# The shared expert's two layers move from a stage of their own into the combine stage

## The reference, cut to what matters

```python
def _expert_ffn(x, w1, b1, gate, w2, b2):
    h = jax.nn.gelu((x @ w1 + b1) * gate, approximate=False)
    return h @ w2 + b2
x = hidden_states
...
combine = jnp.sum(jax.nn.one_hot(topk_i, E, dtype=x.dtype) * topk_p[..., None], axis=-2)
moe = jnp.zeros_like(x)
for e in range(E):
    moe = moe + combine[..., e:e + 1] * _expert_ffn(x, w1[e], b1[e], gate[e], w2[e], b2[e])
shared = _expert_ffn(x, sw1, sb1, sgate, sw2, sb2) * jax.nn.sigmoid(shared_weight)
y = moe + shared
mu = jnp.mean(y, axis=-1, keepdims=True)
var = jnp.var(y, axis=-1, keepdims=True)
return (y - mu) * jax.lax.rsqrt(var + LN_EPS) * ln_g + ln_b
...
x = x + jnp.tanh(g_ffn[0]) * _L0_ffn_ref(_layernorm(x, axis=-1), ...)
```

## Time and profile before

| | before |
|---|---|
| median of three runs | 966.99 us (965.0 to 969.73) |
| the profiled execution, its own time | 970.94 us |
| its span | 968.9 us |
| PE busy | 701.2 us (72%) |
| VectorE (DVE) busy | 747.8 us (77%) |
| ACT busy | 539.0 us (56%) |
| POOL busy | 500.2 us (52%) |
| mean granted TensorE clock | 0.900 of full |

### The profile page before, as it was taken

The page is one execution under the profiler, slowest core; times in us unless marked ns, Lnnn a source line. Parts: engine busy times, 40 slices in busy tenths (PEclk is TensorE's granted clock), DMA queues, the critical chain, the costliest instruction groups (busy, mean ns, idle before and its releaser), DMA issues. The chain is left out here.

```text
span 968.9 us, 25824 instructions
## 1 busy us (share of the span) xinstructions
PE 701.2 (72%) x7850; PEld 563.9 (58%) x7851; DVE 747.8 (77%) x2277; ACT 539.0 (56%) x1099; POOL 500.2 (52%) x438
## 2 busy tenths in 40 slices
PE   2689788777788778787863469999999999990000
PEld 1456555555555555555541458899999999880000
DVE  5698999899989999988964388666665666654998
ACT  2777666756676665865531134455555556552654
POOL 5455567666666666666551692155455555541000
PEclk9999999999999999999885599999999999996555
DMA  4212112222122220300011711122222222225552
GB/s 115 63 39 51 45 50 52 67 62 54 35 65 62 62 54 33 92 26 15 29 40 39 238 36 38 31 68 74 68 74 68 73 69 70 70 68 140 155 150 87
DMA packets 90404, 66.19 MB, mean 68 GB/s; under 512 B 17008, under 2 KB 79728, under 8 KB 90352
## 3 DMA queue, kind: packets, MB, share of 16 engines
q1 hardware_dynamic: 69152, 35.49, 14.7%
q0 software_dynamic: 8448, 17.45, 5.5%
q10 hardware_dynamic: 12752, 12.58, 3.9%
HBM read 38.21 MB, written 23.09 MB: 63 GB/s over the span
## 5 line engine op out<-in xcount | busy, mean ns | idle before, releaser
L1277 POOL DMA_INDIRECT expert_results<-y,dest x136 | 135.3, 995 | 155.4 <-DVE y L1244 109.4
L1099 ACT ACTIVATE hT<-bank,b1g_c,gate_c 128x256 f32<-128x256 f32 x272 | 138.6, 563 | 112.6 <-PE bank L76 111.4
L834 POOL TENSOR_TENSOR prob<-prob,mx 128x1024 f32<-128x1024 f32 x64 | 121.6, 1900 | 148.1 <-DVE mx L536 148.0
L166 POOL DMA_INDIRECT expert_lists<-xn,slots x128 | 124.7, 974 | 67.1 <-issue 30.6
L1041 PE MATMUL bank<-w,hT 128*128 x1088 | 136.1, 278 | 7.4 <-issue 6.8
L366 PE MATMUL bank<-kbd,qg 128*64 128x256 f32 x1024 | 135.5, 405 | 5.5 <-DVE prob L529 3.1
L1041 PEld LDWEIGHTS bank<-w,hT 128*128 128x128 f32 x1088 | 127.0, 191 | 15.0 <-issue 15.0
L762 ACT ACTIVATE PT<-bank 128x512 f32<-128x512 f32 x128 | 70.8, 592 | 85.0 <-PE bank L377 77.9
L383 PE MATMUL bank<-w_att,aT 128*128 128x128 f32 x128 | 33.1, 343 | 94.3 <-issue 65.4
L529 DVE TENSOR_TENSOR prob<-bank,mask 128x512 f32<-128x512 f32 x128 | 85.8, 672 | 17.8 <-PE bank L366 16.0
L366 PEld LDWEIGHTS bank<-kbd,qg 128*64 128x64 f32 x1024 | 70.5, 144 | 46.0 <-issue 16.4
(11 more groups left out here) (176 smaller groups left out, 1639.5 us busy)
## 6 DMA issues: line engine op xcount, KB each, us to landing
rows<-expert_lists SPq DMA_DIRECT2D x70, 130.0 KB
yin<-expert_results SPq DMA_DIRECT2D x16, 512.0 KB, 5.3
x_all<-in_x SPq DMA_DIRECT2D x16, 256.0 KB
ctx_in<-in_ctx SPq DMA_DIRECT2D x16, 256.0 KB
pad_k<-in_mask_BxS_ik SPq DMA_DIRECT2D x16, 256.0 KB
xn2T<-x2T ACTq DMA_DIRECT2D x16, 256.0 KB
out<-res ACTq DMA_DIRECT2D x7, 512.0 KB, 4.7
expert_results<-y,dest POOLq DMA_INDIRECT x136
```

Source lines behind the costliest of these rows:

```text
L166: po.indirect_dma_start(lists[:, :], bass.IndirectOffsetOnAxis(ap=m.slots[:, par, t, k:k + 1], axis=0), m.xn2[:, par, t, :], None).then_in ...
L834: po.tensor_tensor(ps, ps, mx[:, u, :].unsqueeze(2).broadcast_to([P, H, S]), ALU.subtract).then_inc(subbed, 1)
L1099: ac.activation(hT[:, par, c, :], h_ps[par][c // 2][:, (c % 2) * SL:(c % 2 + 1) * SL], ACT.Gelu, bias=b1g_c[:, c, bass.ds(e, 1)], scale=ga ...
L1277: po.indirect_dma_start(results[:, :], bass.IndirectOffsetOnAxis(ap=dest[:, par, h, :], axis=0), y[:, par, h, :], None).then_inc(sent[par] ...
```

## The change

The shared expert leaves the `experts` block. In `combine`, PE computes its first layer from `xn2T` and `sw1` in plain float32 (one product where there were three), ACT the Gelu, and PE the second layer into four PSUM banks (`sy_ps`), which `share` reads in place of `xn2T`. The shared expert's second bias is added to the eight experts' biases instead (once, on `b2_row`; a token's two weights sum to one). The last bias is added to `x_all` by VectorE, two quads in each of the first eight expert steps (`add_bias`, now on VectorE), so VectorE's list has eight steps written out ahead of its loop. The wait for `w1` is split in two halves.

```diff
-        def iterations(eng, body):
+        def iterations(eng, body, head=1):
             n = eng.value_load(pairs[0:1, 0:1], min_val=TOK // SL, max_val=(T - 3) // 2)
-            body(0, 0, 0)
-            body(1, 1, 0)
-            with eng.Fori(1, n) as i:
+            for i in range(head):
+                body(i * 2, 0, i)
+                body(i * 2 + 1, 1, i)
+            with eng.Fori(head, n) as i:
...
-            for q in range(4):
-                table(q)
-                split_tokens(q + 2, q % 2)
-                keep(q, q % 2)
+            for part in range(4):
+                table(part)
             ve.wait_ge(biases_in, 48)
             ve.tensor_tensor(b1g_c[:, :, :], b1g_c[:, :, :], gate_c[:, :, :], ALU.mult).then_inc(biases_ready, 1)
...
+            ve.tensor_tensor(b2_row[:, :, :], b2_row[:, :, :], sb2_row[:, :].unsqueeze(1).broadcast_to([P, E, D]),
+                             ALU.add).then_inc(biases_ready, 1)
+            for es in range(E):
+                ve.wait_ge(w1_in[2 * es // E], 16)
+                split(ve, (w_split, lambda: ve.wait_ge(w_split, es * 2 + 1)), w1[:, es, 0, :].bitcast(F32R),
+                      w1[:, es, 1, :].bitcast(F32R), w1[:, es, 1, :])
...
+                if isinstance(t, int) and t < HEAD:
+                    for q in range(t * NQ // HEAD, (t + 1) * NQ // HEAD):
+                        add_bias(q)
...
+                ve.tensor_tensor(xs, xs, m.ln_row[:, 1, :].unsqueeze(1).broadcast_to([P, QT, D]), ALU.add)
+            iterations(ve, body, HEAD // 2)
...
-            with po.Fori(0, NQ) as q:
-                add_bias(q)
...
+        @block.tensor
+        def _(pe):
+            def hidden(q):
+                for c in range(SC):
+                    if q >= 2:
+                        pe.wait_ge(sh_gelued, (q - 2) * SC + c + 1)
+                    pe.matmul(sh_ps[q % 2][c][:, :], sw1[:, c * P:(c + 1) * P], xn2T[:, q * QW:(q + 1) * QW],
+                              start=True, stop=True).then_inc(sh_done, 1)
+            def shared(q):
+                pe.wait_ge(sh_gelued, q * SC + SC)
+                if q >= 4:
+                    pe.wait_ge(acc_step, (q - 4) // 2 * A_STEPS + (q % 2 + 1) * QT)
+                for t in range(QT):
+                    for c in range(SC):
+                        last = pe.matmul(sy_ps[q % 4][:, t * D:(t + 1) * D], hs[:, q % 2, c, t * P:(t + 1) * P],
+                                         sw2[:, c, :], start=(c == 0), stop=(c == SC - 1))
+                last.then_inc(sy_done, 1)
+            hidden(0)
+            for q in range(NGR * 2):
+                if q + 1 < NGR * 2:
+                    hidden(q + 1)
+                shared(q)
...
-                                        in1=shared[:, (g * GT + t) * D:(g * GT + t + 1) * D],
+                                        in1=sy_ps[(g * 2 + t // QT) % 4][:, t % QT * D:(t % QT + 1) * D],
...
+            def gelu(q):
+                if q >= 2:
+                    ac.wait_ge(sy_done, q - 1)
+                for c in range(SC):
+                    ac.wait_ge(sh_done, q * SC + c + 1)
+                    ac.activation(hs[:, q % 2, c, :], sh_ps[q % 2][c][:, :], ACT.Gelu, bias=scols[:, 2, c:c + 1],
+                                  scale=scols[:, 0, c:c + 1]).then_inc(sh_gelued, 1)
+            for g in range(2):
+                gelu(g * 2)
+                gelu(g * 2 + 1)
+                weigh(g)
             for g in range(NGR):
+                if g + 2 < NGR:
+                    gelu(g * 2 + 4)
+                    gelu(g * 2 + 5)
                 scale(g)
```

More of the change, by code:

```diff
@@ L978, in _ @@
             ident = cst[:, C_ID:C_ID + P]
[L981 to L1011, removed]
             def turn(t, par, i):
@@ L1064, in _ @@
             halves = [slice(k * E // 2, (k + 1) * E // 2) for k in range(2)]
-            for es in halves:
-                ac.dma_start(w1[:, es, 1, :], a["w1"][es].rearrange("e d f -> d e f")).then_inc(w1_in, 16)
+            for k, es in enumerate(halves):
+                ac.dma_start(w1[:, es, 1, :], a["w1"][es].rearrange("e d f -> d e f")).then_inc(w1_in[k], 16)
             for es in halves:
                 ac.dma_start(w2[:, es], a["w2"][es].rearrange("e (c f) d -> f e c d", f=P)).then_inc(w2_in, 16)
[L1069 to L1084, removed]
+            ac.wait_ge(biases_ready, 2)
             ac.wait_ge(table_ready, 1)
@@ L1171, in table @@
                     ve.tensor_copy(ends[:, :], count[:, :]).then_inc(table_ready, 1)
-            for q in range(4):
-                table(q)
-                split_tokens(q + 2, q % 2)
-                keep(q, q % 2)
+            for part in range(4):
+                table(part)
             ve.wait_ge(biases_in, 48)
             ve.tensor_tensor(b1g_c[:, :, :], b1g_c[:, :, :], gate_c[:, :, :], ALU.mult).then_inc(biases_ready, 1)
-            first = max(4, NQ - 2 - E)
-            for q in range(4, first):
-                split_tokens(q + 2, q % 2)
-                keep(q, q % 2)
-            ve.wait_ge(w1_in, 32)
-            es = 0
-            for q in range(first, NQ - 1):
-                if q + 2 < NQ:
-                    split_tokens(q + 2, q % 2)
-                keep(q, q % 2)
-                while es < E and (q == NQ - 2 or es * (NQ - 2 - first) < E * (q + 1 - first)):
-                    split(ve, (w_split, lambda: ve.wait_ge(w_split, es * 2 + 1)), w1[:, es, 0, :].bitcast(F32R),
-                          w1[:, es, 1, :].bitcast(F32R), w1[:, es, 1, :])
-                    es += 1
+            ve.wait_ge(shared_scaled, 4)
+            ve.tensor_tensor(b2_row[:, :, :], b2_row[:, :, :], sb2_row[:, :].unsqueeze(1).broadcast_to([P, E, D]),
[4 more added lines that the diff above has]
+                      w1[:, es, 1, :].bitcast(F32R), w1[:, es, 1, :])
             ve.wait_ge(w_split, 2 * E)
@@ L1290, in combine @@
     TOK = NT * P
-    x_all, shared, weight, ln_row = m.x_all, m.xn2T, m.weight, m.ln_row
+    SC = FS // P
+    x_all, xn2T, weight, ln_row = m.x_all, m.xn2T, m.weight, m.ln_row
+    sw1, sw2, scols, banks = m.sw1, m.sw2, m.scols, m.banks
     out_rows = out.rearrange("b s d -> (b s) d")
@@ L1304, in combine @@
         res = sb("res", [P, 2, GT, D])
+        hs = sb("hs", [P, 2, SC, QW])
+        sh_ps, sy_ps = [banks[0:2], banks[2:4]], banks[4:8]
+        sh_done, sh_gelued, sy_done = (sem("c_" + n) for n in ("sh_done", "sh_gelued", "sy_done"))
         y_in = [sem(f"y_in{i}") for i in range(2)]
```

48 lines of the change are left out of this document (11 added, 37 removed).

## The result

The changed kernel takes 941.09 us (median of 4 executions, 938.25 to 952.71). The kernel before took 968.36 beside it on the same chip (965.0 to 973.96). The difference of the medians is 27.3 us. The profiled execution took 941.31 us by its own time, with a span of 938.8, against 970.94 and 968.9 before. The forecast was 947.6 in a range of 937 to 961.

A forecast was written before the change was run, and what follows sets the result against it. PE was taken to bound the expert steps and VectorE `combine`. The terms -31.4 + 1.5 + 4 + 6.5 = -19.4 us took the median from 966.99 to 947.6 us, range 937 to 961.

The forecast's parts named there:

- Start of the expert steps: Ahead of the expert steps: the first product comes at 584.1 us against 615.48, -31.4 us.
- VectorE's splits block POOL's scatters: Ahead of the expert steps: eight splits each hold up a scatter, pads 4.9 us later, 952.5 us; chance 6%.
- PE cold at the start: First expert steps: PE, idle since attention, begins them at half clock, +1.5 us, from 0.5 to 3.
- The last bias: First eight expert steps: two additions per step on VectorE make steps of 4.33 us, +4 us, from 1 to 9.8.
- Combine, steady state: Groups of `combine`: PE's products and ACT's Gelus fit beside VectorE's 9.60 us, and `share` from PSUM costs nothing, 0 us.
- Head of combine: Start of `combine`: VectorE's fifth share waits for PE's cold first quads, +6.5 us, from 2 to 14.
- PE at half clock in `combine`: Rival in `combine`: PE sets the group at 15.0 us in place of 9.60, 985 us; chance 7%.
- ACT as the bound: Rival in `combine`: Gelus come late behind PE and cost 2.4 us a group, 965 us; chance 10%.
- That the change saves nothing there: Rival at the expert steps' start: the chain through SP ends just as late, 979 us; chance 2%.
- VectorE stopped again: Rival at the head of `experts`: VectorE's unexplained stop grows, the start loses 8 to 12 us more, 958 us; chance 10%.
- The 4.9 us that no row explained: Head of `experts` before: VectorE's wait ended at 559.08, though PE's second layer was over at 554.2.
- VectorE still waits over 10 us between attention and the first step: Between attention and the first expert step: a VectorE wait over 10 us would show the prediction wrong.

The follow-up runs named there:

- third set: Follow-up runs on one chip, the same as the first set's, beside the kernel before (median 944.44 us); the change itself was not run.
- bias run: The changed kernel with the last bias back on GpSimd and one pair of VectorE's steps written out; 969.68 us in the first set, 916.47 in the third set.
- run with late splits: The changed kernel with VectorE's splits of `w1` held until the pads are ready (one wait); 969.03 us, ratio 0.989 to the kernel before.
- first set: Follow-up runs on one chip beside the kernel before (median 986.29 us), on the bias, the shared expert, the splits and the written-out head.
- second set: Follow-up runs on one chip beside the kernel before (median 965.39 us); the only set with the change unaltered, at 942.73 us, ratio 0.975.
- last run: The changed kernel with pads ahead of the scatters, last-but-one quad's scatters at the end of attention, and last bias on GpSimd; 915.73 us, ratio 0.970.

## Why the prediction was right, point by point

**Start of the expert steps: -31.4 forecast, -31.75 measured** from the first scatter to the first product. In the third set the distance from the first scatter to the first `y` was 84.66 in the kernel before and 54.52 in the bias run, -30.1. The chain was read rightly, POOL's scatters and pads, then SP, with some terms that cancel. The pads were 0.8 us later behind the first scatter (27.60 for 26.77): the scatters took 2.2 us longer beside the splits, the `tensor_scalar` group 1.4 less (3.19; 4.57 was its time before). From SP's first rows to the first product it took 3.81 us, where 2.3 + 2.88 = 5.2 were forecast: before, a second layer of 1.95 us stood between PE's transposes and the first product. The marks that were named came as forecast, shifted by attention's 2.0 us: first pad 567.8 (565), first rows 581.9 (579), first product 585.7 (582 to 588).

**VectorE's splits block POOL's scatters** was a rival at +4.9 us. Its mechanism is real but smaller: 1.3 to 1.9 us by the run with late splits, with single scatters of 1.48 and 1.66 us for 0.96 beside splits. Two others of 1.35 and 1.24 us stand clear of the splits (544.36, 559.98), so something else slows them too.

**PE cold at the start: +1.5 forecast, 0 measured in the changed kernel.** Its first products do run at half clock, 0.21 us apart for 0.12 later. But before, the first step had gaps of 1.00 and 0.29 us in which PE waited for VectorE and ACT, and the slower products fill these. In the other profiles without the stage, first product to first `y` is 6.9 to 8.1 us, so 0 to 1.2.

**The last bias: +4 forecast, 2.5 measured** for the first eight steps (32.3 against 29.8). VectorE's step was forecast at 4.33 us and is 4.01. Against the later steps of its own profile (29.4) it is 2.9, and 4.65 at the pace of the third set. What it costs is 4.01 less the step that PE could do, so this term depends on that pace: the eight take 32.1 to 32.7 us in every profile that has it.

**Combine, steady state: 0 forecast, 0 measured.** Group 9.60 us as before, and without the shared expert the stage is no shorter than in the kernel before (94.32 us, 94.59). `share` with its operand in PSUM takes 340 ns (x64), with SBUF it took 344. The Trainium skill (VectorE: DVE Perf Modes, on the TRN2 errata) gives PSUM the larger fixed part; this kernel's own instruction now shows that it isn't there for this form.

**Head of combine: +6.5 forecast, +3.4 measured.** The mechanism is as forecast, the fifth share waits for PE. PE started with SP's loads, as forecast (847.62, 847.57), and 6.0 us behind the last `y`, as SP's loads did before. The size was off in two terms. From there to the end of quad 1's second layer 12.4 us were forecast and 10.7 measured (858.36): the first layers of two quads took 5.29 us for 6.6, because the granted clock was at full after 3.6 us of work (851.2) and not after 5.6, and the later pieces follow each other 0.1 to 0.2 us closer. So the first group is 3.2 us late for 4.9. And of the further 1.6 us for the second group 0.3 came: the additions L1295 of groups 0 and 1 stand 7.64 us apart (859.62, 867.26), 7.31 before, because PE's next four pieces took 7.0 us for 7.7 and VectorE needed them 6.8 us after the first group's, not 6.1.

**Not in the sum: -3.7 us in the steps**, made of +2.5 from the bias and -6.2 from faster later steps (29.3 to 29.4 us for eight, 29.8 before). The third set shows the same step in both codes, and the first the same undisturbed pair of steps. So this most likely belongs to the executions, not to the change; at the pace of the first profiles it isn't shown, as the kernel before wasn't profiled at it again. What makes the pace of a set is open. In the first set waits of VectorE at `rT` are named `remote` (17.6 us, six times, longest 3.7, in the 100 us from 700 on, without the shared expert), in the third there are none and PE is busy over 99.9%.

**The other rivals.** PE at half clock in `combine`: its clock is 1.00 over the group shown and it is done before VectorE needs it. Between groups the clock did fall to 0.5 once in mid-stage (892.6 to 895.7), which the prediction named as a sign of being wrong; PE had enough lead, and the groups stayed at 9.6 us. ACT as the bound: it keeps 1.26 us of 9.60 idle, and `scale` comes 0.30 us after its input. That the change saves nothing there: PE no longer keeps landed rows waiting.

VectorE stopped again: its longest wait ahead of the splits is 1.09 us, on a DMA. The 4.9 us that no row explained are not in every execution: in the third set the kernel before waits 11.88 us there and goes on at 546.26, 0.03 us behind PE's second layer (542.48 + 3.75). The first 7.4 of the old 16.06 us, up to that layer's start at 550.43, came through ACT, whose first Gelu started at 548.84, behind the issue of a weight load (539.03, 8.42 us) and a table load. The sign "VectorE still waits over 10 us between attention and the first step" did come by its words (24.29 us), but behind all of VectorE's work, for rows; it was worded too widely.

**The sum.** With these parts alone, -31.75 + 2.5 + 3.4 = -25.9 us were the change's own in the first pair of profiles; -19.4 was forecast. The 6.5 us between are the head (3.1), the bias (1.5), the cold start (1.5) and the earlier steps (0.4), each of which came out better than priced. The rest of the span's -30.1 is +2.0 in attention and -6.2 of pace, which aren't the change's: without them the measured time would have been some 4 us nearer to the forecast. In the third set the parts are, with the run without the shared expert for the first two and the bias run for the last, -31.1 + 4.0 + 3.7 = -23.4 us, and the second set's medians differ by 22.7. So 23 to 26 us are the change's own. The ways to be wrong were judged well in the main, but one chance doesn't fit its time: ACT as the bound at 965 us was counted as faster than 962.2.

## What to carry to other kernels

A stage is best moved to where its engine is idle under another engine's bound. Here PE's work went under VectorE's group of 9.60 us and cost only the first group's start. Before pricing such a move, find the last wait behind the stage and follow its queue: here 22 us of landed rows lay unused, and the next limit, pads that stood behind the scatters although SP needed them first, together with scatters that could be sent earlier, gave another 16.5 us. When work is moved between VectorE and GpSimd, look at which SBUF instructions then run side by side; two gains that are measured apart need not add.

## What was not expected of the hardware

- GpSimd's additions and VectorE's float32 conversions in SBUF hold each other up, but not evenly. In the kernel before they took turns: 23.85 us for the 16 additions for 19.54 alone, with conversions of at most 1.55 us beside them (0.42 alone). In the last run one conversion stood for all 16 additions, 20.16 us. The Trainium skill (SBUF — State Buffer, on who interferes with whom) describes an exclusive lock on a shared port that is held for one instruction. By that rule the conversion would have waited for one addition of some 1.2 us; why it waited for 16 is open. The memset above, 2.05 us with 2.07 beside it, agrees with the rule. That the loop is the cause is read from this one profile and from the runs without the overlap; GpSimd's loop was not moved in this version.
- The same kernel before took 986, 965 and 944 us in the three sets, from the pace of the expert steps and from the end of attention: the first scatter stood at 528.5 us in the third set's profile of it and at 542.4 in the first set's, which has the written-out head. One code's times are up to 4% apart between sets, so a difference between sets says nothing about code.
